# A merged stage of two recurrences: TensorE's extra products while both of them run

## The chip, the cores and the metric

The kernel runs on one NeuronCore of one Trainium2 chip. The metric is the device time of one execution in microseconds, 4663.28 us as the median of three. TensorE (PE, its weight loads PEld), VectorE (DVE), ScalarE (ACT) and GpSimd (POOL) work beside each other, each in the order of its own instructions, and wait for one another by semaphores.

## What is computed

A residual stream `x` of 32 sequences of 128 positions and 128 features goes through four layers of conditioned attention and feed-forward blocks. This stage computes three pieces of it: the leaky recurrence of layer 0 that reads `x`, the feed-forward block of eight experts on the recurrence's states, which is added to `x`, and the LSTM of layer 1 that reads the new `x`:

```python
def step(h, z_t):                                  # leaky recurrence
    gate = sigmoid(h @ Wh.T + z_t @ Wz.T + b)
    h_new = tanh(h * (1.0 - alpha) + gate * z_t)
    return h_new, h_new

x = x + ffn(hs)        # per token: layernorm, 8 experts of 32 hidden units, gelu, top 1 by router

def step(carry, xp_t):                             # LSTM, xp_t = x_t @ Wx + b
    prev_h, prev_c = carry
    h_bar = xp_t + prev_h @ Wh                     # 512 columns: i, f, o, g
    next_c = f * prev_c + i * g
    next_h = o * tanh(next_c)
    return (next_h, next_c), next_h
```

## The kernel before

The program is a row of stages with a barrier between them. The stage of this change, `leaky_experts_lstm_stage`, is the second and takes the span from about 377 to 773 us. All matrices lie with features on the 128 partitions; a recurrent state is a tile of 128 x 32, one column for each of the 32 sequences. One f32 product of the code is two pairs of weight load and MATMUL in the trace.

The three pieces run as one wave of steps `c`, 144 in all. The leaky recurrence does position `c` in the steps 0 to 127. The experts take its states in tiles of four positions, some steps later. The LSTM does position `c - 16` (`FIRST_LAG`) in the steps 16 to 143. So both recurrences run in the 112 steps 16 to 127. The steps 0 to 27 and 124 to 143 are written out (`known`), the 96 between them are a loop of six times 16 steps.

On TensorE a step is, in this order: `lstm`, four products of 128 x 32 with the LSTM's recurrent weights, behind a wait for the last LSTM state (L919); `leaky`, one such product (L911); in one step of four each `hidden` (L943, 392 columns: router scores, centred states and hidden units of a tile), `turn` (three transposes, L952 and L953) and `output` (L960, L961); `lstm_pre`, a quarter of the input products of the next four steps (L934, with strided columns of `x`), at the first of four with the bias (L931, 512 columns); `leaky_pre` at the last of four (L905). Last come the extra products of `fill_clock` (L761): 128 rows of zeros in bf16 by 512 columns, into PSUM bank 7, which nobody reads in this stage. Nothing waits for them but what stands behind them on TensorE. Before the first step there are 28 of them (`FIRST_FILLS`).

ScalarE does, per step, the tanh of the four LSTM gates (L1012), the leaky gate's tanh (L1017), the cell's tanh (L1022) and the leaky state (L1026). VectorE does the cell (L1122, L1124, L1127, L1129), the leaky gate (L1139), the new LSTM state (L1134, read by the next step's L919) and the leaky mix (L1145). GpSimd runs three Newton steps for the experts' layernorm. SyncE loads the weights of the next stage at the start.

Of the kernel before, what the change touches and what calls it, by code (L numbers as in the profile page):

```python
# [93 lines left out]
@contextmanager  # L94
def stage_scope(nc):

    before = nc.snapshot_sems()
    with ExitStack() as ctx:
        yield ctx
    nc.clear_and_free_semaphores(nc.allocated_since(before))  # L100
    nc.all_engine_barrier()  # L101
# [656 lines left out]
def fill_clock(pe, core, n, bank=FILL):  # L758

    for _ in range(n):  # L760
        pe.matmul(core.ps[:, bank, :], core.fill[:, 0:P], core.fill[:, :], start=True, stop=True)  # L761
# [37 lines left out]
def leaky_experts_lstm_stage(core, next_load):  # L799
# [6 lines left out]
    HIDDEN, ROUTED, UNITS, TURNED, OUTPUT = 4, 5, 7, 9, 10  # L806
    NEWTON = 12
    I32, B16 = mybir.dt.int32, mybir.dt.bfloat16
    FILLS = (2, 3, 2, 3)
    with stage_scope(nc) as ctx:  # L810
        sb = lambda n, shape, t=F32: ctx.enter_context(nc.sbuf_tensor(f"first_{n}", shape, t))
        sem = lambda n: nc.alloc_semaphore("first_" + n)
# [29 lines left out]
        def tile_at(st, lag, known):  # L842

            if (st.c - lag) % 4 or known and not 0 <= (st.c - lag) // 4 < NB:
                return None
            return st.every4(lag)

        def leaky_runs(st, known):
            return not known or st.c < P

        def lstm_runs(st, known):
            return not known or FIRST_LAG <= st.c < FIRST_LAG + P
# [47 lines left out]
        def _(pe):  # L900
            wait_pack(pe, core, 1)

            def leaky_pre(quad, base):
                lo = 2 + quad % 2
                pe.matmul(ps[:, lo, 0:AHEAD * NB].rearrange("p (t b) -> p t b", t=AHEAD), w("WzT"),  # L905
                          positions(core.x, base, AHEAD), start=True, stop=False, skip_group_check=True)

            def leaky(st):
                past(pe, s["leaky_ready"], st.s())
                lo = st.c % 4 * NB  # L910
                pe.matmul(ps[:, 2 + st.c // 4 % 2, lo:lo + NB].unsqueeze(1), w("WhT"), leaky_state(st), start=False,  # L911
                          stop=True, skip_group_check=True).then_inc(s["leaky_z_done"], 1)

            def lstm(st):
                past(pe, s["h_ready"], st.s(-FIRST_LAG))
                state = const("cond").unsqueeze(1) if st.c == FIRST_LAG else positions(core.a, st.s(-FIRST_LAG - 1))
                for z in range(4):
                    lo = (z * AHEAD + st.c % 4) * NB
                    last = pe.matmul(ps[:, st.c // 4 % 2, lo:lo + NB].unsqueeze(1), v("Wh", z * P, P), state,  # L919
                                     start=False, stop=True, skip_group_check=True)  # L920
                last.then_inc(s["z_done"], 1)

            def lstm_pre(st):
                k, bank = st.c % 4, (st.c // 4 + 1) % 2
                if k == 0:
                    pe.wait_ge(s["stored"], st.every4(FIRST_LAG - 4) + 1)
                    if st.c == FIRST_LAG - 4:
                        wait_pack(pe, core, 2)
                        pe.wait_ge(s["halved"], 3)
                        pe.wait_ge(s["bias_ready"], 4)  # L930
                    pe.matmul(ps[:, bank, :], bias_w[0:68, :], pick[0:68, :, :, :], start=True, stop=False,  # L931
                              skip_group_check=True)
                out = ps[:, bank, k * AHEAD * NB:(k + 1) * AHEAD * NB].rearrange("p (t b) -> p t b", t=AHEAD)
                pe.matmul(out, v("Wx", k * P, P), positions(core.x, st.s(4 - k - FIRST_LAG), AHEAD), start=False,  # L934
                          stop=False, skip_group_check=True)

            def hidden(st, tile):
                pe.wait_ge(s["leaky_ready"], st.s())
                past(pe, s["unit_ready"], tile)
                past(pe, s["scores_ready"], tile)  # L940
                if st.c == HIDDEN:
                    pe.wait_ge(s["folded"], 15)
                pe.matmul(ps[:, ALL, 0:NE + P + NH], ring_tile(st, HIDDEN), rhs[:, :], start=True, stop=True).then_inc(  # L943
                    s["hidden_done"], 1)

            def turn(tile):
                pe.wait_ge(s["masked_ready"], tile + 1)
                pe.wait_ge(s["hot_ready"], tile + 1)
                past(pe, s["gelu_ready"], tile)
                past(pe, s["gt_ready"], tile)  # L950
                for j in range(2):
                    pe.transpose(ps[:, TURN, j * P:(j + 1) * P], um[:, j * P:(j + 1) * P], const("ident"))  # L952
                pe.transpose(ps[:, TURN, NH:NH + P], g[:, :], const("ident")).then_inc(s["turn_done"], 1)  # L953

            def output(tile):
                pe.wait_ge(s["gelu_ready"], tile + 1)
                pe.wait_ge(s["gt_ready"], tile + 1)
                past(pe, s["stored"], tile)
                for j in range(2):
                    pe.matmul(ps[:, OUT, 0:P], w("W2", j * P, P), ht[:, j * P:(j + 1) * P], start=(j == 0), stop=False)  # L960
                pe.matmul(ps[:, OUT, 0:P], w("b2"), gt[:, :], start=False, stop=True).then_inc(s["out_done"], 1)  # L961

            def fold(st):
                if st.c == 1:
                    for e in range(NE):
                        lo = 32 * (e % 4)
                        last = pe.matmul(ps[lo:lo + 32, TURN, e // 4:e // 4 + 1], w("W1", e * 32, 32),
                                         w("ln_bias", e, 1), start=True, stop=True)
                    last.then_inc(s["shifts_done"], 1)
                    pe.wait_ge(s["folded"], 8)  # L970
                    pe.matmul(ps[:, ALL, 0:NH], const("center"), scaled[:, :], start=True, stop=True).then_inc(
                        s["centred_done"], 1)
                if st.c == 3:
                    pe.wait_ge(s["folded"], 14)
                    pe.matmul(ps[:, ALL, 0:NH], ones[:, :], diag[:, :], start=True, stop=True).then_inc(
                        s["rows_done"], 1)

            def body(st, known):
                if lstm_runs(st, known):
                    lstm(st)  # L980
                if leaky_runs(st, known):
                    leaky(st)
                tile = tile_at(st, HIDDEN, known)
                if tile is not None:
                    hidden(st, tile)
                tile = tile_at(st, TURNED, known)
                if tile is not None:
                    turn(tile)
                tile = tile_at(st, OUTPUT, known)
                if tile is not None:  # L990
                    output(tile)
                if not known or 0 <= st.c // 4 * 4 + 4 - FIRST_LAG < P:
                    lstm_pre(st)
                if st.c % 4 == 3 and (not known or st.c + 1 < P):
                    leaky_pre(st.c // 4 + 1, st.s(1))
                both = leaky_runs(st, known) and lstm_runs(st, known)
                fill_clock(pe, core, FILLS[st.c % 4] if both else 4)
                if known:
                    fold(st)

            pe.wait_ge(core.filled, 1)
            leaky_pre(0, 0)
            fill_clock(pe, core, FIRST_FILLS)
            run(pe, body)

        @block.scalar
# [2156 lines left out]
```

## Time and profile before

| | us |
|---|---|
| median of three runs (lowest to highest) | 4663.28 (4662.86 to 4663.63) |
| the profiled execution | 4662.41 |
| its span, first to last instruction | 4660.6 |
| PE busy | 4309.6 (92%) |
| PEld busy | 3214.5 (69%) |
| DVE busy | 2494.8 (54%) |
| ACT busy | 1859.3 (40%) |
| extra products L761 on PE, 932 of them | 284.8 |

The mean granted clock of TensorE over the span is 0.959 of full speed. TensorE's products are pipelined and their ends are modelled, so that it is marked busy also where it waits for the rest of a product; the starts of instructions tell more than the busy time. A line of the view by time merges neighbouring instructions of one line: `x8` are eight of them, and the length goes from the first start to the last end.

### The profile page before, as it was taken

How to read it: one execution, taken by the hardware profiler on the slowest of the kernel's cores; microseconds unless marked ns; L12 is line 12 of the kernel's file. 1: busy time of each engine (PE TensorE's matmuls, PEld its weight loads, DVE VectorE, ACT ScalarE, POOL GpSimd, SP SyncE). 2: the span in 40 equal slices, each digit the busy share in tenths (PEclk: the TensorE clock that was granted, in tenths of full speed). 3: DMA queues.
4: the chain of work that ended last, by engine and by line, in shares of the span. 5: the costliest groups of instructions: out<-in, count | busy, mean ns of one | idle time of the engine just before them, and what ended most of it. 6: DMA issues, size and time to landing. Idle time of an engine off the chain costs nothing. (4 is left out here: it accounts for less than half of the span.)

```text
span 4660.6 us, 118083 instructions
## 1 busy us (share of the span) xinstructions
PE 4309.6 (92%) x41087; PEld 3214.5 (69%) x41087; DVE 2494.8 (54%) x7506; ACT 1859.3 (40%) x4669; POOL 761.1 (16%) x3314
## 2 busy tenths in 40 slices
PE   6999999999998999998799999999997887889998
PEld 4556777777876888886355787787875555566666
DVE  5775664555554777776555444666666563421111
ACT  4433443333331444444233222666664452333333
POOL 1111220000001555554122000111111210000000
PEclk9999999999998999998699998999998997989999
DMA  1000000000000000000000000000000100000000
GB/s 53 0 0 25 0 0 25 0 0 0 0 0 10 1 2 1 1 1 1 33 1 0 3 0 0 3 3 3 3 3 2 52 0 1 0 1 0 0 0 18
DMA packets 3080, 28.73 MB, mean 6 GB/s; under 512 B 320, under 2 KB 832, under 8 KB 1216
## 3 DMA queue, kind: packets, MB, share of 16 engines
q1 hardware_dynamic: 2768, 24.81, 1.4%
q8 instruction: 167, 2.74, 0.2%
q14 instruction: 145, 1.19, 0.1%
HBM read 22.71 MB, written 2.10 MB: 5 GB/s over the span
## 5 line engine op out<-in xcount | busy, mean ns | idle before, releaser
L2231 DVE SCALAR_TENSOR_TENSOR experts_acc<-banks,experts_gate,experts_acc 128x128 f32<-128x128 f32 x512 | 144.2, 345 | 461.7 <-PE banks L2177 460.6
L2177 PEld LDWEIGHTS banks<-weights,experts_hidden 128*128 128x128 f32 x2560 | 303.3, 192 | 55.0 <-issue 49.7
L604 DVE TENSOR_REDUCE cells_row_max<-banks 128x4 f32<-128x512 f32 x384 | 238.5, 684 | 161.6 <-PE banks L397 161.6
L2177 PE MATMUL banks<-weights,experts_hidden 128*128 128x128 f32 x2560 | 305.2, 275 | 0.0
L761 PE MATMUL banks<-clock_fill 128*128 128x512 bf16 x932 | 284.8, 394 | 7.4 <-DVE wave_bias_parts L1612 7.4
L2450 ACT ACTIVATE experts_hidden<-banks,weights 128x512 f32<-128x512 f32 x256 | 175.8, 687 | 268.5 <-PE banks L2447 265.2
L1412 PEld LDWEIGHTS banks<-act_a,weights 128*128 128x128 f32 x2032 | 256.1, 196 | 25.6 <-DVE act_a L1670 18.0
L2447 PE MATMUL banks<-act_a,weights 128*128 (+1 forms) x512 | 262.3, 643 | 0.7 <-ACT experts_hidden L2450 0.3
L1412 PE MATMUL banks<-act_a,weights 128*128 (+1 forms) x2032 | 248.7, 281 | 10.8 <-DVE act_a L1670 10.7
L541 ACT ACTIVATE cells_probs<-banks 128x512 f32<-128x512 f32 x384 | 198.2, 603 | 95.0 <-PE banks L437 90.0
L604 DVE TENSOR_REDUCE attn_row_max<-banks 128x4 f32<-128x512 f32 x256 | 159.0, 684 | 134.8 <-PE banks L397 134.8
L1539 ACT ACTIVATE wave_hidden_turned<-banks,weights 128x128 f32<-128x128 f32 x512 | 192.4, 457 | 93.6 <-PE banks L1485 93.4
L2636 ACT ACTIVATE lin_context_turned<-banks 128x256 f32<-128x256 f32 x128 | 49.0, 383 | 404.0 <-PE banks L2588 404.0
L541 ACT ACTIVATE attn_probs<-banks 128x512 f32<-128x512 f32 x384 | 198.2, 603 | 29.5 <-PE banks L437 29.5
L1473 PEld LDWEIGHTS banks<-weights,wave_hidden_turned 128*128 128x128 f32 x1024 | 141.0, 203 | 82.6 <-issue 82.2
L2447 PEld LDWEIGHTS banks<-act_a,weights 128*128 128x128 f32 x512 | 91.2, 201 | 132.2 <-ACT experts_hidden L2450 95.1
L2669 DVE TENSOR_TENSOR lin_masked<-banks,constants 128x512 f32<-128x512 f32 x128 | 88.5, 692 | 173.8 <-PE banks L2568 173.8
L919 PEld LDWEIGHTS banks<-act_a,weights 128*128 128x128 f32 x1016 | 126.0, 192 | 45.2 <-issue 30.3
L1473 PE MATMUL banks<-weights,wave_hidden_turned 128*128 128x128 f32 x1024 | 145.7, 288 | 11.2 <-DVE x_res L1757 10.0
L761 PEld LDWEIGHTS banks<-clock_fill 128*128 128x128 bf16 x932 | 111.0, 124 | 63.5 <-issue 16.1
L2535 PE MATMUL banks<-lin_src,weights 128*128 128x128 f32 x1024 | 141.4, 281 | 4.1 <-ACT lin_features L2629 2.0
L2578 PEld LDWEIGHTS banks<-lin_value,lin_masked 128*128 128x128 f32 x1024 | 135.1, 193 | 6.7
(522 smaller groups left out, 9904.5 us busy)
## 6 DMA issues: line engine op xcount, KB each, us to landing
weights<-in_p SPq DMA_DIRECT2D x1, 2894.5 KB, 17.2
weights<-in_p SPq DMA_DIRECT2D x1, 2894.0 KB, 9.2
weights<-in_p SPq DMA_DIRECT2D x2, 1364.0 KB, 7.1
x_res<-in_x SPq DMA_DIRECT2D x1, 2048.0 KB, 14.9
out_x<-x_res SPq DMA_DIRECT2D x1, 2048.0 KB, 6.3
weights<-in_p SPq DMA_DIRECT2D x1, 1836.0 KB, 10.9
weights<-in_p SPq DMA_DIRECT2D x1, 1835.5 KB, 6.9
weights<-in_p SPq DMA_DIRECT2D x1, 1344.5 KB, 9.8
```

What stands on the lines that cost most here:

```text
L541: act.activation(pt[:, g, :], ps[:, KEYS + g, :], ACT.Exp).then_inc(s["exp_done"], 1)
L604: dve.tensor_reduce(mt[:, 4 * g:4 * g + 4], bank, AX_X, ALU.max).then_inc(s["max_ready"], 1)
L761: pe.matmul(core.ps[:, bank, :], core.fill[:, 0:P], core.fill[:, :], start=True, stop=True)
L1412: last = pe.matmul(ps[:, bank + j, lo:lo + NB].unsqueeze(1), packs[j]("Wh", z * P, P), state, start=False, stop=True, skip_group_check=True)
L1473: last = pe.matmul(ps[:, OUT, j * P:(j + 1) * P], ht[:, q % 2, j * P:(j + 1) * P], w("W2", (4 * q + j) * P, P), start=True, stop=True)
L1539: last = act.activation(ht[:, q % 2, j * P:(j + 1) * P], ps[:, TURN, j * P:(j + 1) * P], ACT.Gelu, bias=w("be1", e, 1), scale=w("g1", e, 1))
L2177: last = pe.matmul(ps[:, 2 + e % 2, t * P:(t + 1) * P], hs[lo:lo + n, (tile + f) % slots, t * P:(t + 1) * P], out_rhs(e, f, lo, n), start= ...
L2231: last = dve.scalar_tensor_tensor(out=acc[:, t, :], in0=ps[:, 2 + e % 2, t * P:(t + 1) * P], scalar=g[:, t, e:e + 1], in1=acc[:, t, :], op ...
L2447: return pe.matmul(ps[:, bank, :], w("W1", j * P, P), core.a[:, tok(c * CHUNK, CHUNK)], start=True, stop=True)
L2450: return act.activation(out, ps[:, bank, :], ACT.Gelu, bias=w("b1", j, 1))
L2535: last = pe.matmul(ps[:, QK, (2 * a + t) * P:(2 * a + t + 1) * P], w(name, (2 * st.m + a) * P, P), x, start=True, stop=True)
L2578: last = pe.matmul(ps[:, SUMS, h * (DH + 1):(h + 1) * (DH + 1)], sm[:, st.m % 2, half, a, :], vt[:, st.m % 4, h, :], start=True, stop=True)
```

## The change

In the steps where both recurrences run no extra product is issued any more. In all other steps of the stage, those of one recurrence alone, there are four as before; the ones at the stage's start stay too. The table of counts goes.

```diff
@@ leaky_experts_lstm_stage
-    FILLS = (2, 3, 2, 3)
@@ body(st, known) on TensorE
                 if st.c % 4 == 3 and (not known or st.c + 1 < P):
                     leaky_pre(st.c // 4 + 1, st.s(1))
-                both = leaky_runs(st, known) and lstm_runs(st, known)
-                fill_clock(pe, core, FILLS[st.c % 4] if both else 4)
+                if not (leaky_runs(st, known) and lstm_runs(st, known)):
+                    fill_clock(pe, core, 4)
                 if known:
                     fold(st)
```

## Rows read from the trace of the kernel before

**Rows 1.** stretches: start:end, length, busy of PE, PEld, DVE, ACT, POOL, PEclk, DMA share, GB/s
```profile
560.00:620.00 60.00, 59.92 (x389) 46.82 (x390) 35.93 (x202) 24.50 (x107) 13.68 (x70) 1.00 0.00 0
767.50:773.00 5.50, 5.11 (x16) 2.47 (x14) 1.58 (x10) 1.01 (x4) 0.00 (x0) 0.50 0.01 3
1501.00:1504.00 3.00, 3.00 (x13) 2.48 (x13) 0.64 (x3) 0.60 (x1) 1.78 (x9) 0.50 0.00 0
1505.00:1508.00 3.00, 3.00 (x22) 2.48 (x22) 2.27 (x11) 1.74 (x7) 1.31 (x7) 1.00 0.03 5
3860.00:3880.00 20.00, 20.00 (x96) 20.00 (x95) 0.00 (x0) 0.00 (x0) 0.00 (x0) 0.50 0.00 1
```

**Rows 2.** the same view for L761 alone: the merged steps; busy of PE and PEld
```profile
418.93:729.08 310.15, 80.73 (x281) 30.88 (x280) 1.00 0.00 0
```

**Rows 3.** order of time on TensorE: start, length, instruction; first merged step, first after
```profile
418.93 0.97 PE L919 MATMUL banks<-constants,weights 128*128 128x32 f32 x8
...
729.08 1.08 PE L919 MATMUL banks<-act_a,weights 128*128 128x32 f32 x8
```

**Rows 4.** groups by form, 460 to 710 us: count | busy us, mean ns | idle before, releaser
```profile
L919 PE MATMUL banks<-act_a,weights 128*128 x717 | 94.7, 282 | 0.3
...
L761 PE MATMUL banks<-clock_fill 128*128 128x512 bf16 x224 | 64.5, 385 | 0.0
...
L1012 ACT ACTIVATE first_gates_tanh<-banks 128x128 f32<-128x128 f32 x90 | 24.9, 277 | 60.8 <-PE banks L919 60.8
```

**Rows 5.** order of time, loop steps from 559.83 to 570.96 us
```profile
559.83 1.08 PE L919 MATMUL banks<-act_a,weights 128*128 x8
...
561.45 0.61 PE L905 MATMUL banks<-x_res,weights 128*128 x2
...
561.89 0.83 PE L761 MATMUL banks<-clock_fill 128*128 128x512 bf16 x3
...
563.72 0.91 PE L943 MATMUL banks<-rst_router_centre_hidden,first_leaky_states 128*128 128x392 f32 x2
...
564.47 0.38 PE L931 MATMUL banks<-first_gate_pick,first_bias_parts 68*128 68x512 bf16 x1
...
565.11 0.61 PE L761 MATMUL banks<-clock_fill 128*128 128x512 bf16 x2
...
568.21 1.08 PE L919 MATMUL banks<-act_a,weights 128*128 x8
...
570.96 1.08 PE L919 MATMUL banks<-act_a,weights 128*128 x8
```

**Rows 6.** order of time, the last steps of the stage, 761 to 771 us
```profile
761.12 1.08 PE L919 MATMUL banks<-act_a,weights 128*128 128x32 f32 x8
...
762.24 0.28 ACT L1012 ACTIVATE first_gates_tanh<-banks 128x128 f32<-128x128 f32 x1 [1.49 <-PE banks L919]
...
763.70 1.08 PE L919 MATMUL banks<-act_a,weights 128*128 128x32 f32 x8 [0.63 <-DVE act_a L1134]
...
768.99 1.91 PE L919 MATMUL banks<-act_a,weights 128*128 128x32 f32 x8
...
770.71 1.89 PE L761 MATMUL banks<-clock_fill 128*128 128x512 bf16 x4
770.94 0.28 ACT L1012 ACTIVATE first_gates_tanh<-banks 128x128 f32<-128x128 f32 x1 [2.32 <-PE banks L919]
```

**Rows 7.** order of time on TensorE, the later merged stage, 1501 to 1508 us
```profile
1501.54 1.91 PE L1473 MATMUL banks<-weights,wave_hidden_turned 128*128 128x128 f32 x8
1503.24 1.06 PE L1485 MATMUL banks<-constants,wave_units 128*128 128x128 f32 x4
1504.10 0.62 PE L1401 MATMUL banks<-x_res,weights 128*128 128x128 f32 x2
...
1506.45 1.05 PE L1473 MATMUL banks<-weights,wave_hidden_turned 128*128 128x128 f32 x8
1507.34 0.60 PE L1485 MATMUL banks<-constants,wave_units 128*128 128x128 f32 x4
```

## The prediction

> **What bounds the kernel now.** I read the slices of the span first, then stretches of this stage, then its groups of instructions by form, then single steps in the order of time. In the merged stage TensorE is marked busy for 59.92 of 60 us, at a granted clock of 1.00 (2.4 GHz) [rows 1]. That busy time is not the bound by itself: the extra products alone are 80.73 us of the 310.15 us from the first product of the LSTM recurrence, at 418.93, to the first step after the merged ones, at 729.08 [rows 2, 3]. The wait that ends last in a step is another one: ScalarE's tanh of the gates (L1012) was preceded by 60.8 us of idle time in 250 us, all of it ended by the L919 products [rows 4].
>
> A step is a ring. L919 starts at 568.21 and the next one at 570.96 [rows 5]: 2.75 us, of which 1.12 lie between L919's start and the tanh (762.24 - 761.12 [rows 6]) and 1.63 on ScalarE, VectorE and the hand-overs. The extra products stand behind everything else of the step and mostly fill the time in which TensorE waits for the new state. They touch the ring in one step of four, the one with L943 and L931: there the pair of 0.61 us starts at 565.11 and runs past the new state. Four steps take 570.96 - 559.83 = 11.13 us [rows 5] instead of 4 x 2.75 = 11.00.
>
> So TensorE's part of the ring is eight narrow products with their weight loads. 112 steps run both recurrences: 24 groups of four in the loop (24 x 11.13 = 267.1 us) and 4 groups written out, which have the remaining 43.0 us, 10.76 each.
>
> **What the change removes.** In the 112 merged steps the 2 + 3 + 2 + 3 products of 512 bf16 columns per four steps go: 280 (the trace puts 281 starts into that stretch, one of them of the step before [rows 2]). The four per step where one recurrence runs alone, and the 28 at the start, stay. No wait, semaphore, DMA or other engine's instruction changes. The direct gain is small: 11.13 - 11.00 = 0.13 us for each loop group, and 10.76 - 4 x 2.58 = 0.44 us for each written-out one (2.58 us is the step where nothing delays it and the loop's register work is absent: 763.70 - 761.12 [rows 6]). 24 x 0.13 + 4 x 0.44 = 4.9 us, if all else stays.
>
> **What goes with them: the clock.** The end of this stage shows the clock fall [rows 6]. In its last steps a step has eight L919 products and four extra ones. The eight still take 1.08 us at 763.70 and 1.91 at 768.99, and from 767.5 on the clock is 0.50 (1.2 GHz) [rows 1], although four wide extra products were in each of these steps. A merged step without the extra ones has the same eight L919, two L911, two strided L934 and, by turns, L943 with L931, three transposes, six products of L960 and L961, or two of L905. Some of these steps have nothing wide at all. A second row says that being busy is not enough: from 3860 to 3880 TensorE runs narrow products with a weight load for each, without a gap, 20.00 us busy of 20.00, and the clock is 0.50 throughout [rows 1]. L919 and L911 are of that kind (32 columns behind each load). So I expect the clock to fall within the first merged steps, and not to come back while both recurrences run, since a slower step spreads the same products over more time.
>
> The Trainium skill speaks against this. "TensorE: Matmul & The Clock Gate", section "Why this matters for your kernels", asks only that TensorE is not left idle for long between bursts; without the extra products its idle stretches here would be near one microsecond, so by that rule the clock holds, and the time is that of rival A. The trace does not bear it out as sufficient: 0.50 in a stretch without any idle.
>
> **What the low clock costs.**
> - The ring. At full clock L919 to tanh is 762.24 - 761.12 = 1.12 us; at the low one 770.94 - 768.99 = 1.95 [rows 6]. That is +0.83 a step: 3.58 in the loop, 3.41 where written out. ScalarE and VectorE keep their times (L1012 is 0.28 in both rows).
> - TensorE's work in a step, which was covered and now is not always. A product of up to 128 contiguous columns with its weight load goes from 0.89/8 = 0.11 us (1506.45 to 1507.34, clock 1.00) to 1.70/8 = 0.213 (1501.54 to 1503.24, clock 0.50) [rows 1, 7]. A 512-column bf16 product goes from 0.22 (0.61 for two less 0.39 for one [rows 4, 5]) to twice that, 0.43; 1.89/4 = 0.47 [rows 6] is its upper bound. L934 and L905 have strided columns: two take 561.89 - 561.45 = 0.44 up to the next product at full clock [rows 5]; the like of them, L1401, has 0.62 for two at the low clock [rows 7], as L905 has 0.61 at full clock: 0.44 at both. L943 takes 564.47 - 563.72 = 0.75 now [rows 5]; at the ratio of the eight L919, 1.91/1.08, it would be 1.33, and doubled 1.50; I take 1.40.
> - By kind of step: with L943 and L931, 10 x 0.213 + 1.40 + 0.43 + 0.44 = 4.40; with three transposes 2.13 + 0.64 + 0.44 = 3.21; with L960 and L961 2.13 + 6 x 0.213 + 0.44 = 3.85; with L905 3.01. Where that is over the ring's time, it counts instead.
>
> A loop group then takes 4.40 + 3.58 + 3.85 + 3.58 = 15.41 us (now 11.13), a written-out one 4.40 + 3.41 + 3.85 + 3.41 = 15.07 (now 10.76). 24 x 4.28 + 4 x 4.31 = 120 us. The clock needs some steps to fall, about 7 us at the old pace: -3. Behind the merged part 16 steps run with four extra products each. If the clock came back at once they would cost nothing. If it never did, the 15 steps from 729.08 to 768.99, 39.9 us, would be 12 x (1.70 + 0.44 + 4 x 0.43) + 3 x 3.41, and 6.5 for L943, L931, L952, L953, L960 and L961: 63, so +23. The first of them has L943, L931, L934 and four extra products in a row, the widest run of the stage, so I take an early return, +5. Sum: 120 - 3 + 5 = +122.
>
> Here too a rule of the Trainium skill stands against the rows: the same page, section "LDWEIGHTS (loading the stationary operand)", gives a load of 128 columns 107 ns without regard to the array's clock. By it (an estimate) eight loads would be 0.86 us at either clock, the ring would hardly lengthen, and the time would be near rival A's. The trace differs: the eight L919 took 1.08 us at full clock and 1.91 at the low one.
>
> **The rivals.**
> - A, not slower: the clock holds. L943, L931, L934 and L960 in every group may be enough; no row shows merged steps bare. It decides from the point at which the clock never falls between 419 and 729: then the 4.9 us alone stand, 4658.4. Against it are the end of the stage and the busy but slow stretch. Chance 0.08.
> - B: the clock alternates; it falls in the thin steps and returns behind L943 and L931. Low for half of the time it costs 0.5 x 120 = 60, 4723. Against it: at the low clock a group is 15.4 us long and its widest run of products under 2.3 us. Chance 0.12.
> - C: as forecast, and the low clock also lasts through the tail: 120 - 3 + 23 = +140, 4803. For it: at the end of the stage steps with four extra products fell and did not recover. Chance 0.2.
> - The forecast, with an early return: 0.58. Something not seen at all: 0.02.
>
> That the change does nothing is excluded: the 280 products are in the trace, and the condition that drops them is fixed when the program is built.
>
> **How the numbers follow.** The profiled execution took 4662.41 us (span 4660.6), 0.9 under the median; I put the sum on the median: 4663.3 + 122 = 4785. Forecast and C together hold 0.78 and reach from about 4768 (L943 at its lower bound, -2; a later fall; a return now and then) to 4812 (L943 at its upper bound, +3, wide products at 0.47, the tail at +23). The range takes in a part of B: 4720 to 4812. A measurement of this kernel can tell about 0.2%, 9.3 us, from no change. Faster by more than that: 0.01. Within it (A): 0.08. Slower: 0.91.
>
> **What would show it.** Right: a granted clock near 0.5 over most of the stretch from 425 us on; the mean of L919's products up from 282 ns [rows 4] toward 390; 1.95 us from L919 to L1012's tanh; steps of 3.58 us where nothing blocks, and L919 right behind L934 after the step with L943; 652 products of L761 instead of 932; other stages unchanged to a microsecond. Wrong: the clock at 1.00 with steps of 2.75 (A), or a clock that changes every ten microseconds (B). If steps last 3.58 without the two longer ones, the second term was over-sized, by 28 x (0.82 + 0.27) = 30 us at most.

## The result and the profile after

The changed kernel takes 4781.81 us (median of 4, 4777.47 to 4786.02) against 4663.45 us: the ratio is 1.0251, with a 95% interval of 1.0234 to 1.0269. That is 118 us slower; 4785 had been forecast, in a range of 4720 to 4812. The profiled execution has a span of 4781.0 us, 120.4 over that of before.

The slices of the span, busy share of each engine and the granted clock in tenths (the kernel after):

```profile
PE   7998999999999899999889999899998797889998
PEclk9997555899999999999889999899999898989999
```

The first line is nearly full here as elsewhere. The second has a hole of three slices at 5: in this stage TensorE ran at the lower of its two levels. The stretches of the stage show when (start:end, length, busy us of PE, PEld, DVE, ACT and POOL, granted clock, DMA share, GB/s):

```profile
386.00:420.00 34.00, 28.26 (x159) 16.87 (x158) 18.74 (x85) 11.04 (x42) 8.17 (x38) 1.00 0.01 3
420.00:431.00 11.00, 10.35 (x68) 8.00 (x67) 6.62 (x38) 4.50 (x20) 2.82 (x15) 1.00 0.00 0
432.00:854.00 422.00, 412.47 (x1706) 369.49 (x1706) 187.71 (x1044) 133.12 (x548) 68.30 (x354) 0.50 0.00 0
855.00:888.00 33.00, 30.73 (x188) 20.94 (x187) 11.51 (x68) 7.03 (x28) 1.29 (x7) 1.00 0.00 1
```

The clock holds while the first four merged steps run, falls as the fifth starts, and comes back only behind the merged steps. The products of L918 in the low stretch, as a group (count, busy us, mean ns, idle before):

```profile
L918 PE MATMUL banks<-act_a,weights 128*128 x752 | 171.3, 392 | 8.7 <-DVE act_a L1133 5.7
```

Their mean is 392 ns, where it was 282 [rows 4]. In the whole trace there are 652 products of L761 instead of 932. The order of time around the two ends of the merged part and at the stage's end, on TensorE, is (start, length, instruction; L918 is the L919 of before, since a line of the kernel has gone):

```profile
421.11 0.97 PE L918 MATMUL banks<-constants,weights 128*128 128x32 f32 x8
...
428.81 1.08 PE L918 MATMUL banks<-act_a,weights 128*128 128x32 f32 x8 [0.16 <-DVE act_a L1133]
...
431.40 1.92 PE L918 MATMUL banks<-act_a,weights 128*128 128x32 f32 x8 [0.35 <-DVE act_a L1133]
...
843.82 1.92 PE L918 MATMUL banks<-act_a,weights 128*128 128x32 f32 x8 [0.48 <-DVE act_a L1133]
...
847.87 1.89 PE L761 MATMUL banks<-clock_fill 128*128 128x512 bf16 x4
849.55 1.75 PE L918 MATMUL banks<-act_a,weights 128*128 128x32 f32 x8
...
853.93 1.34 PE L918 MATMUL banks<-act_a,weights 128*128 128x32 f32 x8
...
888.35 1.53 PE L918 MATMUL banks<-act_a,weights 128*128 128x32 f32 x8 [0.64 <-DVE act_a L1133]
...
892.97 2.05 PE L2534 MATMUL banks<-lin_src,weights 128*128 128x128 f32 x8 [1.38 <-POOL lin_src L2519]
```

From the first merged step to the first after them it is 843.82 - 421.11 = 422.7 us, where it was 310.15 [rows 2, 3]: +112.6. The fifteen steps behind them took 888.35 - 843.82 = 44.5 us, where they were 39.9 (768.99 - 729.08 [rows 3, 6]): +4.6. The first merged step came 421.11 - 418.93 = 2.2 us later than before. The next stage's first products started at 773.99 in the kernel before:

```profile
773.99 2.05 PE L2535 MATMUL banks<-lin_src,weights 128*128 128x128 f32 x8 [1.38 <-POOL lin_src L2520]
```

892.97 - 773.99 = 119.0 us of the 120.4 are thus in this stage, 112.6 of them in the merged steps. All other stages together take 1.4 us more.

Two loop steps of after and the start of a third, in the order of time (TensorE, the tanh of the gates and the writing of the state, and two rows of weight loads):

```profile
565.28 1.73 PE L918 MATMUL banks<-act_a,weights 128*128 x8
566.83 0.61 PE L910 MATMUL banks<-first_leaky_states,weights 128*128 128x32 f32 x2
567.05 0.28 ACT L1011 ACTIVATE first_gates_tanh<-banks 128x128 f32<-128x128 f32 x1 [1.87 <-PE banks L918]
567.25 0.77 PE L933 MATMUL banks<-x_res,weights 128*128 x2
567.85 0.61 PE L904 MATMUL banks<-x_res,weights 128*128 x2
568.35 0.21 DVE L1133 TENSOR_TENSOR act_a<-first_tc,first_output_gate 128x32 f32 x1 [0.23 <-ACT first_tc L1021]
...
568.68 1.78 PEld L918 LDWEIGHTS banks<-act_a,weights 128*128 128x128 f32 x8 [0.52 <-issue]
568.69 1.91 PE L918 MATMUL banks<-act_a,weights 128*128 x8 [0.23 <-DVE act_a L1133]
570.41 0.61 PE L910 MATMUL banks<-first_leaky_states,weights 128*128 128x32 f32 x2
570.64 0.28 ACT L1011 ACTIVATE first_gates_tanh<-banks 128x128 f32<-128x128 f32 x1 [1.66 <-PE banks L918]
570.84 1.65 PE L942 MATMUL banks<-rst_router_centre_hidden,first_leaky_states 128*128 128x392 f32 x2
571.93 0.21 DVE L1133 TENSOR_TENSOR act_a<-first_tc,first_output_gate 128x32 f32 x1 [0.23 <-ACT first_tc L1021]
572.29 0.63 PE L930 MATMUL banks<-first_gate_pick,first_bias_parts 68*128 68x512 bf16 x1
572.72 0.64 PE L933 MATMUL banks<-x_res,weights 128*128 x2
...
572.95 1.81 PEld L918 LDWEIGHTS banks<-act_a,weights 128*128 128x128 f32 x8
573.16 1.73 PE L918 MATMUL banks<-act_a,weights 128*128 x8
```

There are two kinds of step here. At 568.35 VectorE starts to write the state, TensorE has nothing more to start, and L918 starts behind the state: the ring decides. At 571.93 the state is written too, but L942, L930 and L933 still stand ahead, and L918 starts at 573.16, 1.0 us after the state was done (571.93 + 0.21): TensorE's own work decides. ScalarE's tanh takes 0.28 us as before; from L918 to it there are 570.64 - 568.69 = 1.95 us, as in the stage's last step in the kernel before [rows 6].

### The profile page after: what moved, and what is told of

Same layout as the page of the kernel before. It is cut to its first block and busy times, and to the rows that moved or that the text cites. A ratio compares the mean times of both kernels' runs of the same rounds, so it can differ in the third digit from the quotient of the medians.

```text
span 4781.0 us, 117523 instructions
## 1 busy us (share of the span) xinstructions
PE 4418.5 (92%) x40807; PEld 3347.5 (70%) x40807; DVE 2498.1 (52%) x7506; ACT 1869.2 (39%) x4669; POOL 760.7 (16%) x3314
## 5 line engine op out<-in xcount | busy, mean ns | idle before, releaser
L1411 PEld LDWEIGHTS banks<-act_a,weights 128*128 128x128 f32 x2032 | 257.0, 196 | 25.3 <-DVE act_a L1669 17.7
L2446 PE MATMUL banks<-act_a,weights 128*128 (+1 forms) x512 | 262.5, 644 | 0.7 <-ACT experts_hidden L2449 0.3
L1411 PE MATMUL banks<-act_a,weights 128*128 (+1 forms) x2032 | 249.7, 281 | 10.2 <-DVE act_a L1669 10.1
L918 PEld LDWEIGHTS banks<-act_a,weights 128*128 128x128 f32 x1016 | 215.5, 311 | 36.4 <-issue 23.3
L918 PE MATMUL banks<-act_a,weights 128*128 (+1 forms) x1016 | 219.5, 378 | 13.2 <-DVE act_a L1133 9.2
L761 PE MATMUL banks<-clock_fill 128*128 128x512 bf16 x652 | 205.9, 401 | 7.4 <-DVE wave_bias_parts L1611 7.4
L2446 PEld LDWEIGHTS banks<-act_a,weights 128*128 128x128 f32 x512 | 91.2, 201 | 132.3 <-ACT experts_hidden L2449 95.1
```

What stands on the lines that cost most here:

```text
L1411: last = pe.matmul(ps[:, bank + j, lo:lo + NB].unsqueeze(1), packs[j]("Wh", z * P, P), state, start=False, stop=True, skip_group_check=True)
L2446: return pe.matmul(ps[:, bank, :], w("W1", j * P, P), core.a[:, tok(c * CHUNK, CHUNK)], start=True, stop=True)
```

## The experiments

Two theories were at odds. W: the clock follows how much the products stream through TensorE, so removing the wide ones drops it. G: it falls only where TensorE is left idle, so that the wide products matter as fillers of gaps. Besides, the forecast had two prices, the ring and TensorE's own work, and a guess about the tail. All kernels of this section differ from the kernel before in the counts or the form of the extra products alone. The expectation stands behind each edit.

### Narrow products instead of wide ones

```diff
-    FILLS = (2, 3, 2, 3)
+    FILLS = (4, 6, 4, 6)
...
-                fill_clock(pe, core, FILLS[st.c % 4] if both else 4)
+                if both:
+                    for _ in range(FILLS[st.c % 4]):
+                        pe.matmul(core.ps[:, FILL, 0:NB], core.fill[:, 0:P], core.fill[:, 0:NB], start=True, stop=True)
+                else:
+                    fill_clock(pe, core, 4)
```

> The extra products of the merged steps are kept but made narrow: 32 columns instead of 512, and twice as many (4, 6, 4, 6 per four steps instead of 2, 3, 2, 3), so that TensorE is about as busy as in the kernel before and issues more weight loads. Theory W (the clock follows how much the products stream): the clock falls as in the changed kernel, and the narrow products, 0.213 us each at the low clock, lengthen steps on top: 4.47 + 0.85, 3.21 + 1.28, 4.02 + 0.85 and 3.01 + 1.28 us, 18.7 us per four steps against 11.1 before, 28 x 7.5 = +210 and some 5 for the tail, about 4875 us. Theory G (only idle gaps of TensorE let the clock fall): there are fewer gaps than in the changed kernel, the clock holds at 1.00 and the time is within a few us of the kernel before, 4660 to 4668.

4793.87 us, one run. The clock fell as under W and stayed at 0.50 from 432 to 866 us. The size was missed: four steps took 15.9 us, not 18.7. Four of these products, each with a weight load of its own, start within 602.94 - 602.80 = 0.14 us:

```profile
602.80 0.30 PE L999 MATMUL banks<-clock_fill 128*128 128x32 bf16 x4
602.94 1.89 PE L919 MATMUL banks<-act_a,weights 128*128 x8
```

I had priced them like the f32 ones. So short, they also fill few gaps at full clock, and the run does not speak clearly against G. It was done again with products that take the time of the wide ones:

```diff
-                fill_clock(pe, core, FILLS[st.c % 4] if both else 4)
+                if both:
+                    for _ in range(FILLS[st.c % 4]):
+                        pe.matmul(core.ps[:, FILL, 0:NB], w("WhT"), const("cond"), start=True, stop=True)
+                else:
+                    fill_clock(pe, core, 4)
```

> The extra products of the merged steps are as many as before (2, 3, 2, 3), but each is one f32 product of 128 x 32 with the leaky recurrence's weights, two weight loads and two MATMULs of 32 columns: at full clock 2 x 0.11 = 0.22 us, the same length on TensorE as one of 512 bf16 columns. The gaps of TensorE stay what they were in the kernel before. This mends the first narrow kernel, whose products were too short to fill the gaps (it was sized at 0.213 us for each and they cost about a third of that or less). Theory G (gaps decide): the clock holds at 1.00, about 4663 us. Theory W (what the products stream decides): it falls in the first merged steps and stays low; four steps take 4.47 + 0.85, 3.21 + 1.28, 4.02 + 0.85 and 3.01 + 1.28 us, 19.0 us, 28 x 7.9 = +221 and some 5 in the tail, about 4888 us.

4872.38 us, one run. Its merged steps as stretches (the columns as above):

```profile
400.00:425.00 25.00, 21.25 (x125) 15.48 (x127) 13.87 (x64) 9.15 (x37) 5.76 (x28) 1.00 0.00 1
419.00:427.00 8.00, 8.00 (x58) 7.52 (x57) 4.55 (x29) 3.40 (x15) 1.38 (x7) 0.90 0.00 0
426.00:930.00 504.00, 504.00 (x2238) 479.46 (x2238) 185.89 (x1038) 132.36 (x545) 70.09 (x361) 0.50 0.00 0
```

TensorE is marked busy for 504.00 us of 504.00, and the clock was 0.50 all the time. The shortest step of its loop, 4.27 us, is longer than the ring's 3.41, so that TensorE did not wait for the ring either. The clock fell in the third merged step, within a stretch (419 to 427 us) in which TensorE was busy for 8.00 us of 8.00. G is out as a sufficient rule: being busy neither kept the clock nor brought it back. An extra product of this kernel differs from one of the kernel before in more than one way: 32 columns behind a weight load instead of 512, f32 in two passes instead of bf16 in one, and weights and data in place of zeros. The narrow bf16 products of zeros did not hold the clock either, but they left gaps, and wide f32 products were not tried. That the columns are what counts is thus the likely reading, not a shown one. Four steps took 5.15 + 4.37 + 4.69 + 4.27 = 18.5 us (19.0 expected).

### Where the low clock's price lies

One extra product of 512 columns is added to the changed kernel, once in the step with L943, once in the step with L905.

```diff
-    FILLS = (2, 3, 2, 3)
+    FILLS = (1, 0, 0, 0)
```

> As the changed kernel, but one wide extra product in the merged step that has L943 and L931, none in the other three. If the step with L943 is bound by TensorE's own work at the low clock (4.47 us where the ring needs 3.58), the product adds its 0.43 us in each of 28 groups: +12 us on the changed kernel, 4794. If only the ring of the recurrence counts, it adds nothing: 4782. If one product per group is enough to bring the clock back behind L943, the time falls by tens of us.

```diff
-    FILLS = (2, 3, 2, 3)
+    FILLS = (0, 0, 0, 1)
```

> As the changed kernel, but one wide extra product in the merged step that has L905, none in the other three. That step has 3.0 us of TensorE's work at the low clock against a ring of 3.4 to 3.6, so the product's 0.43 us should be covered: 4782 as the changed kernel, at most +3. If every piece of work on TensorE were on the path, it would be +12, 4794.

The second is the clean one. Its ratio to the kernel before is 1.0252 (1.0235 to 1.0269), as the changed kernel's 1.0251. The median is 4790.37 us, with the kernel before at 4670.56 in the same session, 7 us over its value in the session of the changed kernel. Its steps, on TensorE:

```profile
600.48 0.60 PE L761 MATMUL banks<-clock_fill 128*128 128x512 bf16 x1
600.89 1.91 PE L919 MATMUL banks<-act_a,weights 128*128 x8
...
605.36 1.73 PE L919 MATMUL banks<-act_a,weights 128*128 x8
...
608.77 1.91 PE L919 MATMUL banks<-act_a,weights 128*128 x8
...
612.78 1.74 PE L919 MATMUL banks<-act_a,weights 128*128 x8
...
615.78 0.60 PE L761 MATMUL banks<-clock_fill 128*128 128x512 bf16 x1
616.20 1.91 PE L919 MATMUL banks<-act_a,weights 128*128 x8
```

Steps of 605.36 - 600.89 = 4.47, 3.41, 4.01 and 616.20 - 612.78 = 3.42 us: a group of 15.31 us, with the extra product as without. Its 0.43 us lay in time that TensorE had.

The first gave 4777.35 us, ratio 1.0236 (1.0219 to 1.0253), from four executions that spread over 4761.49 to 4789.50; the trace is of the fastest. Its step with L943 took 612.34 - 607.46 = 4.88 us, 0.41 more than the 4.47 without the product, so there the product was on the path. But it did more:

```profile
601.70:628.80 27.10, 26.50 (x110) 23.48 (x109) 11.77 (x65) 8.23 (x34) 4.82 (x26) 0.50 0.00 0
629.00:632.00 3.00, 2.33 (x19) 1.94 (x19) 1.81 (x12) 1.40 (x6) 0.09 (x1) 1.00 0.00 0
632.40:642.50 10.10, 9.85 (x41) 8.48 (x40) 4.63 (x25) 3.21 (x14) 2.21 (x11) 0.50 0.00 0
```

The clock came back for one or two steps behind the widest run of the group and fell again, about twice in three groups. In this execution that gave back more than the product cost: the merged steps took 407.7 us against 422.7. Over the four executions the gain is not shown, since the two ratios' intervals overlap (1.0219 to 1.0253, 1.0234 to 1.0269). This is rival B's mechanism, with one product per group more than the change left. The expectation had it as the third case, with a gain of tens of us; 15 us is the most that a trace shows.

### How many extra products, and where

Six instead of ten, once in the steps that have nothing wide and once in the others:

```diff
-    FILLS = (2, 3, 2, 3)
+    FILLS = (0, 3, 0, 3)
```

> Extra products only in the two merged steps without L943, L960 and L961: 0, 3, 0, 3 per four steps, 6 instead of 10. Theory: what counts is that no run of steps carries too little, so 6 well placed ones hold the clock, the ring is free and the step with L943 loses its delay: 24 x 0.13 + 4 x 0.44 = -4.9 us at best, 4659. If it is the number alone that counts and 6 are too few, the clock falls for most of the stage, and the time is near the changed kernel's, 4770 to 4800. If the clock alternates, between, near 4700.

```diff
-    FILLS = (2, 3, 2, 3)
+    FILLS = (3, 0, 3, 0)
```

> Extra products 3, 0, 3, 0 per four merged steps: the same six as in 0, 3, 0, 3, but in the steps that have L943 and L960 already. Theory (the thin steps let the clock fall): it falls within the first groups and is low for most of the merged steps, with single returns behind the step of L943, whose low-clock length is 4.47 + 3 x 0.43 = 5.8 us; 4770 to 4840. If only the number of extra products counted, it would behave as 0, 3, 0, 3 did: some 60 us at full clock first, then long stretches of either, near 4774.

4774.38 us for the first, 4795.29 for the second, one run each. Stretches of the first:

```profile
385.00:472.00 87.00, 80.31 (x494) 56.70 (x492) 50.72 (x268) 32.88 (x138) 20.11 (x98) 1.00 0.02 9
474.00:585.00 111.00, 111.00 (x448) 94.51 (x449) 45.24 (x255) 32.61 (x135) 15.66 (x78) 0.50 0.00 0
784.00:832.00 48.00, 46.47 (x301) 35.73 (x300) 28.91 (x166) 19.95 (x87) 12.43 (x62) 1.00 0.00 0
```

The merged steps ran some 50 us at full clock, the last 20 of them in the loop, then at the low one for over 300 us with two short returns, and again at full clock for their last 48 us. So one row of instructions can sit at either level. At the low one a group takes 16.8 us (4.31 + 4.35 + 3.86 + 4.25) instead of 11.0, so that the same products are spread more thinly. This agrees with the prediction's argument that a slower group defends the low clock; that the spreading is the reason is not shown. Why the clock came back where it did stays open: the two short returns and the lasting one lie 99 us apart (585.4, 684.4 and 783.4 us), in a loop whose instructions do not change. In the second kernel the clock began to fall at 425.5 us and changed dozens of times; its merged steps were at the low clock for 294 us of 435. Placement changes how the clock behaves. The second kernel has more time at full clock and is not faster: its merged steps take 435 us against 411, since at the low clock the three wide products next to L943 are on the path (a step of up to 5.73 us).

### The tail without extra products

```diff
-                fill_clock(pe, core, FILLS[st.c % 4] if both else 4)
+                fill_clock(pe, core, 4 if st.c < FIRST_LAG and leaky_runs(st, known) and known else 0)
```

> As the changed kernel, and the four extra products in each of the 16 steps behind the merged part are left out too. Theory: what brought the clock back in the first of these steps (855 us, in the changed kernel) was the run of L943, L931, L934 and the extra products. Without them it stays low to the stage's end: the 15 steps take about 4.0 + 14 x 3.4 = 51.7 us instead of 42 to 44.5, and the time is 7 to 10 us over the changed kernel's. Rival: the clock comes back because the leaky recurrence has ended, whatever the extra products do; then the steps take 2.58 us and the time is the changed kernel's or 2 us less.

4793.87 us, one run (that the first narrow kernel has the same figure is chance, the traces differ). The steps behind the merged part (the columns of the stretch as above):

```profile
855.00:894.00 39.00, 28.61 (x119) 25.67 (x118) 10.52 (x62) 6.52 (x26) 0.00 (x0) 0.50 0.00 0
```

The clock never came back in this stage. The fifteen steps took 894.35 - 842.64 = 51.7 us, exactly as expected (44.5 in the changed kernel), and the time was 12 us over the changed kernel's median, in another session; 7 of them are these steps. In the changed kernel, then, the clock would not have come back without the extra products of the tail; the leaky recurrence's end alone does not bring it back.

### Fewer only where they delay

In the loop, the ring's delay in the step with L943 is the one thing that the extra products cost in the kernel before. Two kernels take it away and keep eight or nine products:

```diff
-    FILLS = (2, 3, 2, 3)
+    FILLS = (1, 3, 2, 3)
```

> Extra products 1, 3, 2, 3 per four merged steps: one less in the step that has L943, the only one in which they ran past the new state. Theory: the clock holds at 1.00 and each group of the loop takes the ring's 11.00 us instead of 11.13, as the groups at full clock in the kernel with 0, 3, 0, 3 did: 24 x 0.13 = 3 us and up to 1 us in the written-out steps, -3 to -4 us on the kernel before. Rival: nine are too few somewhere, the clock falls once and stays low for a hundred us, +30 to +110.

```diff
-    FILLS = (2, 3, 2, 3)
+    FILLS = (0, 3, 2, 3)
```

> Extra products 0, 3, 2, 3. At full clock -3 to -5 us on the kernel before. With 0, 3, 0, 3 the clock held for 89 us at a time and then fell for 113; two more in the step of L960 and L961 should make falls rarer or end them. If it holds: 4658 to 4660 against 4663. If it falls as there: 4700 to 4775.

4662.31 us, ratio 0.9989 (0.9980 to 0.9999), and 4661.89 us, ratio 0.9989 (0.9980 to 0.9998), with the kernel before at 4666.37 us in the same session. The second, as stretches and in the order of time:

```profile
421.50:728.09 306.59, 303.98 (x1960) 234.09 (x1958) 186.64 (x1063) 128.08 (x559) 73.01 (x364) 1.00 0.00 0
```

```profile
585.39 1.08 PE L919 MATMUL banks<-act_a,weights 128*128 x8
...
588.25 1.08 PE L919 MATMUL banks<-act_a,weights 128*128 x8 [0.16 <-DVE act_a L1134]
...
591.00 1.08 PE L919 MATMUL banks<-act_a,weights 128*128 x8
...
593.76 1.08 PE L919 MATMUL banks<-act_a,weights 128*128 x8
```

The clock is 1.00 throughout, steps are 2.75 us (one in sixteen, at the loop's own turn, 2.86), and the merged part takes 306.59 us instead of 310.15: -3.6, where 3 to 5 were expected. A last kernel also trims the written-out merged steps and the tail:

```diff
-    FILLS = (2, 3, 2, 3)
+    FILLS, WRITTEN_OUT, TAIL = (0, 3, 2, 3), (0, 3, 1, 3), {P: 1, P + 1: 3, P + 2: 2, P + 5: 3, P + 6: 2}
...
-                fill_clock(pe, core, FILLS[st.c % 4] if both else 4)
+                fill_clock(pe, core, (WRITTEN_OUT if known else FILLS)[st.c % 4] if both else TAIL.get(st.c, 4))
```

> Extra products 0, 3, 2, 3 per four merged steps in the loop, 0, 3, 1, 3 in the written-out merged steps, and behind the merged part 1, 3, 2, 4, 4, 3, 2 and then 4: fewer wherever they were seen to run past the new state (steps 128, 130 and 134 take 3.17, 2.96 and 2.96 us where the ring needs 2.58). If the clock holds as in the kernel with 0, 3, 2, 3: its 3.5 us, and 0.6 + 0.4 + 0.4 us in the tail and 4 x 0.15 in the written-out steps, together -5 to -6 us on the kernel before, 0.1%. Rival: the tail's trimmed steps let the clock fall early; then +3 to +15 us.

4663.00 us, ratio 0.9988 (0.9979 to 0.9997), kernel before 4666.79. In the trace the trimmed steps are at the ring's time:

```profile
730.78 1.09 PE L919 MATMUL banks<-act_a,weights 128*128 128x32 f32 x8
...
733.37 1.09 PE L919 MATMUL banks<-act_a,weights 128*128 128x32 f32 x8
...
735.95 1.09 PE L919 MATMUL banks<-act_a,weights 128*128 128x32 f32 x8
```

2.59 and 2.58 us; the first of them took 3.17 before. But the clock fell earlier at the stage's end, at 765 us (in the kernel with 0, 3, 2, 3 the eight L919 still take 1.08 us at 765.32), and the last steps gave back what these had saved: the fifteen steps take 39.8 us in this kernel and in the one with 0, 3, 2, 3. The rival was right in kind there, and small. All three are faster than the changed kernel, and about 0.1% faster than the kernel before: the intervals lie below 1, the nearest by 0.0001, so that this gain is small and barely clear of the spread. That the clock holds with eight products rests on one profile for each of these kernels and on the runs' times, none of which is over 4670 us.

## Why the prediction was right, step by step

**What bounds the kernel.** The reading of the ring held. With one extra product or none next to L943 four loop steps take 11.0 us, in the kernels with nine and eight, and in the one with 0, 3, 0, 3 while its clock was full. The gain "if all else stays" was put at 4.9 us; the merged part of the kernel with 0, 3, 2, 3 gave 3.6. In its profile the written-out merged steps still hold products that delay (2.76 and 2.62 us), and one loop step in sixteen has 0.1 us more, which I had not seen.

**The fall of the clock.** Right, and at about the step expected: the clock fell between 428.81 and 431.40, where "within the first merged steps" and about 7 us had been said. The 7 us came from no row; it was 431.40 - 421.11 = 10.3 us. Rival A is out, by the result and by the products of 32 columns; with it went the Trainium skill's rule as a sufficient one. "TensorE: Matmul & The Clock Gate", section "Why this matters for your kernels", asks that TensorE is not left idle for long: in 504 us without any idle the clock was 0.50. That the 32 columns are the reason is the likely reading only, as said above. Rival B (the clock alternates) did not come in the changed kernel, and came with one wide product more.

**The ring at the low clock.** 1.95 us from L918 to the tanh, as forecast from the last step of the stage, but only where L918 starts behind the state. The steps that the ring alone decides took 3.41 us in the loop, not the 3.58 that had been named as a sign: all of them stand behind a late step, as the next paragraph says. With no late step before them, written-out steps took the 3.41 forecast for them: from 870 us on, the steps of the tail without extra products take 3.41 or 3.42 us, with 1.92 for the eight. "LDWEIGHTS (loading the stationary operand)" of the Trainium skill's page "TensorE: Matmul & The Clock Gate" gives 107 ns for a load of 128 columns, whatever the clock. At full clock the 0.11 us of a load with its product is near it [rows 7]; at the low one it is (570.41 - 568.69)/8 = 0.215 us, twice that.

**TensorE's own work.** The group was put at 15.41 us and took 15.31 (4.47 + 3.41 + 4.02 + 3.41), but the parts were not the forecast ones (4.40 + 3.58 + 3.85 + 3.58). Behind a step in which TensorE is late, the first weight load of L918 starts 0.21 us before the first product (572.95 and 573.16), where it otherwise starts with it (568.68 and 568.69), and the eight take 1.73 us instead of 1.91. The two steps behind the late ones were therefore 0.17 shorter each than forecast. The late ones were longer, by 0.17 (L959) and by 0.07 (L942). So two errors nearly cancelled in the group, and its 0.1 us of agreement is in part luck. From L942's start to L930's it took 572.29 - 570.84 = 1.45 us, where 1.40 was taken between 1.33 and 1.50.

**Entry and tail.** The entry was put at -3 us; the first group ran at full clock in 10.3 us, 4.8 less than a written-out group at the low one was forecast to take. The tail was put at +5 and measured +4.6; rival C (+23) did not come. It was a guess between two bounds, and that it came so near is luck. The kernel without extra products in the tail bears out a part of its reason: without them the clock stayed low. But it did not come back with the first, widest step of the tail: two steps still ran low, and in the third it rose (1.34 us for the eight at 853.93).

In all, +120.4 us between the two spans against the +122 forecast: +112.6 for the merged part (117 forecast), +4.6 for the tail (5), +2.2 at the stage's start, -0.4 in its last step and +1.4 in all other stages. Of the 4.4 us by which the merged part was over-sized, 2.4 are the 24 loop groups (15.31 for 15.41), 1.8 the entry (4.8 saved where 3 were forecast) and 0.2 the other written-out groups. The 2.2 us at the start are not the change's: the instructions there are the same, and the first merged step's start also differed between the experiments, from 419.07 to 424.44 us, with the clock's level before it: from 380 to 385 us it was 0.86 in the kernel before and 0.64 in the changed one.

## What to carry to other kernels

Products that nobody reads can pay for themselves: here 280 of them, 81 us of TensorE's time, cost about 4 us and save 118, because the stage's own products, most of them narrow, do not keep the clock up alone. Before taking such work away, look for a stretch of the same trace in which similar steps ran at the lower clock, and read the price of the ring there; then take away only those that stand in the way when the wait ends. When the clock is low, add up TensorE's work per step anew, for work that was covered at full clock may no longer be so at half of it.

## What the runs showed of the hardware

- TensorE was marked busy for 504.00 us of 504.00 at a granted clock of 0.50, mostly with weight loads and products of 32 columns. In this case a full busy share does not tell that the clock is full.
- One and the same loop can sit at either clock: with 0, 3, 0, 3 it ran groups of 11.0 us and of 16.8 us, changing over without a change in the loop's instructions.
- At the low clock four bf16 products of 32 columns, each with a weight load, start within 0.14 us. The f32 ones of L918 start 0.215 us apart. I had priced the former like the latter.
- The same eight f32 products with their loads take 1.91 us where the first load starts together with the first product, and 1.73 us where it starts 0.21 us ahead, behind other work of TensorE.
- The time of the kernel before spread over 4654 to 4680 us in the experiments' sessions, against 4662.9 to 4663.6 in its first three runs. The gain of 0.1% above rests on 11 or 12 executions of each trimmed kernel, and the intervals reach up to 0.9997 to 0.9999.
